# Attention and expert kernel: one reduction per tile for the softmax sums, an even spread of the first variances, and a new place for root seeds and slot sums

## The reference

```python
x = x + xattn(layernorm(x), ctx)         # 16 heads of 32, 77 keys per batch
x = x + ffn(layernorm(x), ...)           # 8 experts, top 2, capacity 1024
...
attn = einsum(q, k) * scale; attn = clip(attn, -1e4, 1e4)
attn = softmax(attn, axis=-1)
x = einsum(attn, v) @ Wo + bo
...
m = mean(x); v = var(x); return (x - m) / sqrt(v + eps)
```

## Time and profile before

| what | before |
|---|---|
| median of 3 runs | 1451.1 us (1449.7 to 1451.29) |
| profiled execution | 1449.55 us |
| its span | 1447.8 us |
| TensorE busy (matmul) | 1279.6 us, 88% |
| VectorE busy | 984.2 us, 68% |
| ScalarE busy | 771.1 us, 53% |
| GpSimd busy | 733.1 us, 51% |

### The profile page before, as it was taken

One profiled execution on the slowest core, in us unless ns is written; L12 is line 12 of the kernel. 1 busy time (PEld: TensorE's weight loads), 2 busy tenths in 40 slices (PEclk: granted clock), 3 DMA queues, 4 the chain that ended last, 5 costly groups with the idle time before them and its releaser, 6 DMA issues.

```text
span 1447.8 us, 33073 instructions
## 1 busy us (share of the span) xinstructions
PE 1279.6 (88%) x13587; PEld 741.5 (51%) x13650; DVE 984.2 (68%) x1909; ACT 771.1 (53%) x1208; POOL 733.1 (51%) x784
## 2 busy tenths in 40 slices
PE   6838899878997899887628999999999999999996
PEld 3626666656665666664316444444444444444442
DVE  8768999999889887897875545445554545455421
ACT  4557888767887788877345504234251514334210
POOL 3368888777887778877413333242513223241301
PEclk9879999999999999998868999999999999999998
DMA  7157899968786787787524665755747465654401
GB/s 225 33 122 159 204 254 222 229 180 198 211 224 159 168 186 181 186 197 202 151 55 143 177 166 154 164 161 124 185 111 183 137 155 174 149 145 121 107 15 44
DMA packets 320257, 230.11 MB, mean 159 GB/s; under 512 B 253465, under 2 KB 253849, under 8 KB 320106
## 3 DMA queue, kind: packets, MB, share of 16 engines
q1 hardware_dynamic: 304746, 177.33, 50.1%
q0 software_dynamic: 15360, 50.66, 11.8%
HBM read 120.04 MB, written 50.86 MB: 118 GB/s over the span
## 4 chain that ended last, share of the span: by engine, by line
PE 59%; DVE 22%; POOL 5%; issue 4%; ACT 4%; SPq 2%; DMA 2%; DVEq 0%; ACTq 0%; POOLq 0%
PE ps L1234 23%; PE ps L1220 23%; DVE sm L1488 4%; PE ps L1137 4%; PE ps L1118 3%; PE ps L1067 3%; DVE ps L1459 3%; DVE sd L1471 3%; POOL sd L554 2%; DVE xnT L1454 2%; DMA xs<-x 1%; DVE x L1509 1%; DVE st L1341 1%; PE ps L1090 1%; DVE st6b L1516 1%
## 5 line engine op out<-in xcount | busy, mean ns | idle before, releaser
L1220 PE MATMUL ps<-xT,w1s 128*128 128x512 f16 (+1 forms) x1632 | 335.7, 368 | 1.9 <-DVE xT L1807 1.5
L1234 PE MATMUL ps<-w2s,hT 128*128 128x512 f16 x1536 | 332.8, 379 | 0.0
L851 ACT ACTIVATE hT<-ps 128x512 f16<-128x512 f32 (+1 forms) x136 | 77.8, 572 | 355.9 <-PE ps L1220 355.9
L1220 PEld LDWEIGHTS ps<-xT,w1s 128*128 128x128 f16 x1632 | 160.4, 98 | 175.0 <-issue 1.9
L1234 PEld LDWEIGHTS ps<-w2s,hT 128*128 128x128 f16 x1536 | 150.2, 98 | 181.3
L605 POOL DMA_INDIRECT out_dram<-ys,idx x64 | 71.7, 1121 | 278.3 <-DVE ys L1847 273.8
L1067 PE MATMUL ps<-xnT,wqh 128*128 128x256 f16 x1536 | 194.1, 278 | 2.5 <-ACT partq L747 2.5
L1137 PE MATMUL ps<-woh,oT 128*128 128x512 f16 x768 | 182.3, 387 | 13.0 <-issue 7.0
L1837 DVE SCALAR_TENSOR_TENSOR hT<-ps,hT 128x512 f16<-128x512 f32 (+1 forms) x136 | 88.6, 658 | 137.7 <-ACT hT L851 137.6
L560 POOL TENSOR_TENSOR ph<-sd,ph 128x1232 f16<-128x1232 f32 x64 | 162.4, 2537 | 29.3 <-ACT ph L770 29.0
L1847 DVE SCALAR_TENSOR_TENSOR ys<-ps,gs,og 128x512 f32<-128x512 f32 x64 | 48.0, 750 | 189.8 <-PE ps L1234 189.8
(11 more groups left out here) (226 smaller groups left out, 1864.3 us busy)
## 6 DMA issues: line engine op xcount, KB each, us to landing
xr<-x SPq DMA_DIRECT2D x64, 256.0 KB, 4.0
xrow_dram<-x SPq DMA_DIRECT2D x64, 256.0 KB, 3.7
out_dram<-x SPq DMA_DIRECT2D x64, 256.0 KB, 4.0
stage<-w1T SPq DMA_DIRECT2D x8, 2048.0 KB, 10.7
stage<-w2T SPq DMA_DIRECT2D x8, 2048.0 KB, 9.4
xt<-x SPq DMA_DIRECT2D x59, 256.0 KB, 3.6
xs<-x SPq DMA_DIRECT2D x56, 256.0 KB, 4.2
wqf<-wq SPq DMA_DIRECT2D x1, 1024.0 KB, 7.3
```

What stands on the lines that cost most here:

```text
L1220: ins = pe.matmul(hb[z][:, 0:wide], w1s[e % 2][:, a, k, ic * P:(ic + 1) * P], xT[:, 4 * b + k, cols], start=(k == 0 and i == 0), stop=(k = ...
L1234: ins = pe.matmul(yb[z][:, :], hT[:, a, k, s * P:(s + 1) * P], w2s[e % 2][:, b, k, :], start=(k == 0 and i == 0), stop=(k == 7 and i == 2))
```

## The change

The sums of a tile's exponentials are taken in one instruction over 16 heads instead of two over 8. `stats_at` gives one first variance a pass for passes 3 to 40 (pass 2 has two); before, even passes from 4 to 14 had two, and the last came in pass 34. The seeds for batches 5 to 9 stand between the sum and the reciprocal, not at the end of the pass; batches 2 to 4 keep their place. `add_slots` and `next_batch` stand behind `tx_lo`; before, the one stood ahead of the sum and the other behind `value`. In the loop for the tail only the sum changes.

```diff
--- before.py
+++ after.py
@@ -304,8 +304,7 @@
             if h < 2:
                 return {-7: range(8, 10), -6: range(10, 12), -5: range(12, 13), -4: range(13, 15), -3: range(15, 16),
                         -2: range(16, 18), -1: range(18, 20), 0: range(20, 22), 1: range(22, 24)}[h]
-            first = 24 + h - 2 + min((h - 1) // 2, 7)
-            return range(first, min(first + 1 + (h % 2 == 0 and h < 16), T))
+            return range(23 + h - (h == 2), min(24 + h, T))
 
         def q_bank(G, g):
 
@@ -1479,20 +1478,18 @@
                     s_lim(t)
                     s_sub(t)
 
-            def s_sum(t, half):
+            def s_sum(t):
                 if not 0 <= t < T:
                     return
-                if half == 0:
-                    dve.wait_ge(S["e"], t + 1)
-                hs = slice(8 * half, 8 * half + 8)
-                dve.tensor_reduce(sm[:, t % 2, hs], heads(t)[:, hs, :], AX_X, ALU.add).then_inc(S["sm"], 1)
+                dve.wait_ge(S["e"], t + 1)
+                dve.tensor_reduce(sm[:, t % 2, :], heads(t), AX_X, ALU.add).then_inc(S["sm"], 1)
 
             def s_recip(t):
                 if not 0 <= t < T:
                     return
                 if t >= 2:
                     dve.wait_ge(S["pn"], t - 1)
-                dve.wait_ge(S["sm"], 2 * t + 2)
+                dve.wait_ge(S["sm"], t + 1)
                 dve.reciprocal(rr[:, t % 2, :], sm[:, t % 2, :]).then_inc(S["r"], 1)
 
             def residual(t):
@@ -1913,17 +1910,18 @@
                 if h in (22, 38, 54):
                     route = ranking((h - 22) // 16)
                     steps(route, 1)
-                if H:
-                    add_slots(H)
-                s_sum(h + 5, 0)
-                s_sum(h + 5, 1)
+                s_sum(h + 5)
                 for g in ones_at(h):
                     value(g)
-                if H:
-                    next_batch(H[-1])
+                for b in range(5, len(XB)):
+                    if h == seed_at(b):
+                        steps(norm1(b), 9)
                 steps(route, 4)
                 s_recip(h + 5)
                 tx_lo(h + 11)
+                if H:
+                    add_slots(H)
+                    next_batch(H[-1])
                 residual(h)
                 if h % 2:
                     oe_out(h // 2)
@@ -1933,7 +1931,7 @@
                     xe_out((h + 9) // 2)
                 for t in stats_at(h):
                     ln1_stats(t)
-                for b in range(2, len(XB)):
+                for b in range(2, 5):
                     if h == seed_at(b):
                         steps(norm1(b), 9)
                 if h == -6:
```

## The result

The changed kernel takes 1471.79 us (median of 4 runs, 1471.15 to 1476.57) against 1451.19 (4 runs, 1449.7 to 1455.6): ratio 1.0144, 95% interval 1.0113 to 1.0175. It is slower by 1.4%, some 20.6 us. I had forecast 1456.7 and a range up to 1463. The direction was right; the size was missed by 15 us and lies outside the range. The profiled execution took 1471.34 us (span 1469.6).

What follows compares the result with a forecast made beforehand. VectorE bounds passes 2 to 15, TensorE close behind; a TensorE-ScalarE-VectorE loop bounds 24 to 31 and 41 to 47. Terms -0.4 - 4.3 - 0.5 + 2.9 + 4.0 + 2.7 + 3.0 - 0.3 = +7.1 on 1449.55 gave 1456.7 us, range 1446 to 1463.

Steps and rivals of the forecast that it cites:

- The mechanism and its place: Passes with slots: `xe_mm` waits for `acc`, starting 0.9 us after `tx_lo` starts; `pv_mm` follows at 1.55, 0.8 us later.
- T not earlier: Passes with slots: T, the start of `tx_lo`, stays unchanged because `p_lo` holds `put`; 0.2 to 0.3 us in 28 and 44.
- `top` in pass 40: Pass 40: `next_batch` behind `tx_lo` is held by GpSimd's `p_norm`, a `top` or `acc` of about 2 us; cost +1.5 us.
- passes 24 to 31 and 41 to 47: Two stages led by a TensorE, ScalarE, VectorE loop: slot delays and seeds cost +2.9 us and +2.7 us.
- the delay of `pv_mm` lies beside the variance on VectorE: nothing: Passes 32 to 40: late `pv_mm` costs nothing, 5 x 0.5 if cover fails; stage +4.0 us from variances and `next_batch`.
- passes 48 to 55, +3.0: Passes 48, 50 and 52 give 2.4 us; in pass 54 `xe_mm` starts 2 us later, 0.6 reaching the chain.
- passes 2 to 15, -4.3: One variance a pass relieves VectorE, TensorE then leads at 17.0 us a pair: 122.2 us against 126.5; bounds -7.5 and -2.
- Passes 16 to 23, -0.5: Passes 16 to 23: the single sum saves 0.5 us, with the gain swallowed in 16, 17 and 20 to 24.
- nothing in 17: Pass 17: the moved seeds cost nothing, since routing is held in the same place anyway; bounds -0.5 and +1.5 us.
- early relief: Rival, chance 0.20: faster, 1444.7 us; T comes 0.66 us earlier, paying for `xe_mm`, and passes 2 to 15 give 7.5.
- GpSimd becomes the bound: Rival, chance 0.12: slower, 1461.5 us; TensorE waits 2 us for `oT`, passes 2 to 15 give only -2.
- a draw: Rival, chance 0.18: +2 at most, around 1450.5 us; 14 delays cost 0.3 instead of 0.8 us each, `next_batch` nothing.

Runs made afterwards that it cites:

- b_slots: Kernel before with only `add_slots` and `next_batch` moved behind `tx_lo`; ratio to before 1.016, +23 us.
- b_xeatT: Kernel before with one added wait: in passes with slots `xe_mm` also waits for the reciprocal; ratio to before 1.0043, +6.2 us.
- b_xewait: Kernel before with one added wait: in passes with slots, except pass 54, `xe_mm` also waits for that pass's `xnT`; ratio to before 1.0095, +13.8 us.
- a_putsel: Changed kernel with `put` at the front of VectorE's pass in ten even passes (26 to 32, 40 to 50); ratio to before 1.0087.

## Why the forecast was wrong

**Right.** The mechanism and its place: `xe_mm` released by `acc`, at T + 0.9, `pv_mm` at T + 1.51. T not earlier, since the hold of `put` takes the place of the wait (0.86 us became 2.09; taking the hold away gave 0.65 us). Passes 30 and 31, a pair with neither a stop nor a slow stretch: 19.07 us for 18.36, forecast 19.1. `top` in pass 40: 2.02 us, forecast about 2.

**Right in part by luck:** passes 24 to 31 and 41 to 47, +3.3 and +3.5 for +2.9 and +2.7. Passes 28 and 29 grew by 1.7 us with the stop of 1.66 in them. Passes 42 and 43 grew by 3.9 and 46 and 47 by 2.6, each with a stop, where I had 0.8 a pair; 44 and 45 shrank by 0.3, and pass 41 gave back 2.7 us that pass 40 had lost.

**Wrong: passes 32 to 40, "the delay of `pv_mm` lies beside the variance on VectorE: nothing".** Passes 32, 36 and 38 grew by 4.6 us and 33 and 37 behind them by 1.9. The rest of the 10.3 is pass 40 with `next_batch` (2.8), pass 35 with a variance (1.7) and -0.7 in 34 and 39. Three things were left out. First, T there is set by the routing steps and not by `put` alone, so TensorE had idled 1.2 to 2.6 us for T behind `xe_mm` (in passes 2 to 15 at most 1.4); now it idles 2.2 to 3.0 us ahead of it in 32, 36 and 38. Behind it the mean granted clock fell to 0.54 to 0.57 in windows of 3.5 to 4.7 us in passes 32, 36 and 38, and `pv_mm` with `s_mm` took 3.1 to 4.3 us instead of 1.7 (the 4.3 with the stop of pass 36 in it). VectorE then waited 1.5 to 2.5 us for scores; no variance of 0.8 covers that. Second, that stop. Third, the cover was used twice: I charged the variances 2.5 us for the time that they take and let the same 0.8 us a pass hide the delay. b_slots shows the cost without them: the same 106.2 us.

**Wrong: passes 48 to 55, +3.0 for three delays and pass 54.** For pass 54 I let 0.6 us reach the chain, through GpSimd. Passes 54 and 55 took 4.0 more (pass 56 gives 1.0 back), more than half of the stage's 7.6. The way was another: before, nothing held `pv_mm` there, and the scores were under way when the reciprocal came; now they start 3.2 us behind its end, and VectorE waits 2.31 us for them. Passes 48 to 52 took 3.6 for 2.4: the pauses in 48, 50 and 52 were 2.63, 3.41 and 2.45 us, and in 50 the clock fell. I had taken 0.8 us a pass from pass 46, the one kind in which TensorE's pause is short.

**Wrong: no term for TensorE's stops and for the clock.** The stops of the changed kernel come to 5.9 us, and five of its passes with slots have a slow stretch where before had one. Both can stand beside a wait that is there anyway, so these are not their prices. The kernels with a wait alone were to price them, but they are no ladder: b_xeatT (+6.2) has the delay of pass 54 and none in the others, b_xewait (+13.8, `xe_mm` at T + 0.67) has the delays and not that of pass 54, and b_slots (+23.2) has both, and VectorE's order. My sum had 9 us for the delays and `next_batch` (2.4 + 2.1 + 3.0 and 1.5). That the late slots cost all of the 20.6 us is shown; how it splits between the plain delay, the stops and the clock stays open.

**Mis-sized: passes 2 to 15, -4.3, measured -2.8.** I let TensorE lead at 17.0 us a pair. It is ScalarE as well: VectorE's waits there, kernel after,

```profile
DVE xnT L1453 <- ACT xnT L730: 8.3, 11, 1.7
```

where the earlier trace rows had 2.8. My lower bound of -2 held. **Passes 16 to 23, -0.5, measured +1.2:** the seed of pass 17 was held 1.75 us, for which the forecast had "nothing in 17", and the pass took 0.5 more; pass 16 took 0.6 more, with a `pv_mm` of 1.94 us.

The rivals: "early relief" (0.20) would have come to its first half if `put` had not been held, as a_putsel shows, but the slots would have cost more than it gains all the same (+0.87%). "GpSimd becomes the bound" had the right side and 10 us too little. The sum of "a draw" does not follow from its terms: the forecast's sum had nine delays (6.9 us), not 14, and at 0.3 us each they give 2.7 (or 4.2 for 14), so +1.4 or +2.9 instead of +2. And of the 20 additions of slots, 15 lie in passes 26 to 54; the order of the other five the change leaves alone.

## What to carry to other kernels

A wait moved from behind an instruction to ahead of it is not free because the sum of the waits is the same: small work that ran in TensorE's pause now runs behind it, and besides the delay of each pass the loss is paid in single passes (a stop, a slow stretch, a last pass of another kind) far from where one pass is read. Price a delay in each kind of pass, above all in those where the engine already waits longest and in the first and last that the edit touches, and use each microsecond of cover once. When stage totals agree with a forecast, look at the passes in them too. Before moving an instruction with two SBUF operands on VectorE, look up pass by pass whether GpSimd is in the middle of a long one there; the same move gained 0.6 us in one pass and lost 1.4 in another.
